# Three small edits in a four-layer graph kernel: buffer offsets, the place of a layer norm, and the number format of one matmul

## The reference

```python
x = layernorm(x + L0(x))   # two graph attention layers (4 heads of 256), then h @ Wfc + bfc
x = layernorm(x + L1(x))   # hp = h @ weight; msgs = hp[src] * edge_weight; relu(segment_sum(msgs, dst))
x = layernorm(x + L2(x))   # edge messages of 16 x 32 values, summed by src, then two small linear maps
x = layernorm(x + L3(x))   # relu([x[src], x[dst]] @ W.T + b), summed by src
```

## Time and profile before

| what | value |
|---|---|
| median of 3 runs | 2313.13 us (2309.23 to 2315.16) |
| the profiled execution | 2313.32 us, span 2311.3 us, mean granted clock 0.990 |
| PE, PEld busy | 2244.8 us (97%), 1913.1 us (83%) |
| DVE, ACT, POOL busy | 64%, 44%, 41% |

### The profile page before, as it was taken

The page is one execution under the profiler, slowest core; times in us unless marked ns, Lnnn a source line. Parts: engine busy times, 40 slices in busy tenths (PEclk is TensorE's granted clock), DMA queues, the critical chain, the costliest instruction groups (busy, mean ns, idle before and its releaser), DMA issues.

```text
span 2311.3 us, 36469 instructions
## 1 busy us (share of the span) xinstructions
PE 2244.8 (97%) x12307; PEld 1913.1 (83%) x12307; DVE 1490.6 (64%) x4613; ACT 1020.4 (44%) x2044; POOL 946.3 (41%) x931
## 2 busy tenths in 40 slices
PE   7999999979999999999999999999999999999996
PEld 5878788868899888888999999988887777778785
DVE  7777778744766856665345665267676666677675
ACT  3982112222456622222225665334334665666444
POOL 2017637654222234366632222023545554552542
PEclk9999999989999999999999999999999999999998
DMA  6334566442477657785226665456667777676531
GB/s 207 138 137 136 145 197 201 143 140 95 149 233 251 239 173 267 259 278 201 85 83 214 230 235 197 135 193 215 207 207 232 246 238 236 213 229 209 166 118 64
DMA packets 192415, 435.82 MB, mean 189 GB/s; under 512 B 45607, under 2 KB 74542, under 8 KB 191694
## 3 DMA queue, kind: packets, MB, share of 16 engines
q1 hardware_dynamic: 126954, 249.08, 31.4%
q0 software_dynamic: 65296, 184.67, 25.5%
HBM read 242.68 MB, written 190.96 MB: 188 GB/s over the span
## 4 chain that ended last, share of the span: by engine, by line
PE 71%; DVE 4%; ACT 2%; issue 1%; DMA 1%; POOL 0%; DVEq 0%; ACTq 0%; SPq 0%; POOLq 0%
PE g_h_ps L2563 6%; PE g_h_ps L2580 6%; PE g_h_ps L2565 6%; PE g_h_ps L2564 6%; PE g_h_ps L2581 6%; PE g_h_ps L2582 6%; PE g_h_ps L2605 5%; PE g_h_ps L2607 5%; PE g_h_ps L2606 5%; PE g_t_ps L2542 5%; PE g_h_ps L1744 2%; PE g_h_ps L1742 2%; PE g_h_ps L1743 1%; PE g_sum_ps L989 1%; PE g_sum_ps L990 1%
## 5 line engine op out<-in xcount | busy, mean ns | idle before, releaser
L2697 ACT ACTIVATE g_act_t<-g_t_ps,g_b_col 128x256 f32<-128x256 f32 (+1 forms) x488 | 202.2, 466 | 421.3 <-PE g_t_ps L2542 417.4
L2580 PE MATMUL g_h_ps<-g_x_hi,held_w_hi 128*128 128x256 f32 x1216 | 353.0, 290 | 0.0
L2582 PE MATMUL g_h_ps<-g_x_hi,held_w_lo 128*128 128x256 f32 x1216 | 343.9, 283 | 0.0
L2581 PE MATMUL g_h_ps<-g_x_lo,held_w_hi 128*128 128x256 f32 x1216 | 343.8, 283 | 0.0
L601 DVE CUSTOM_DVE_ANT_0 g_prod<-g_h_sb,g_a_rows 128x256 f32<-128x256 f32 x632 | 224.1, 418 | 80.8 <-ACT g_h_sb L492 73.2
L2605 PE MATMUL g_h_ps<-fc_w_hi,g_x_hi 128*128 128x512 f32 x632 | 272.3, 431 | 3.3 <-DVE fc_z L2982 2.5
L2563 PE MATMUL g_h_ps<-held_w_hi,g_x_hi 128*128 128x512 f32 x656 | 265.2, 404 | 0.0
L2565 PE MATMUL g_h_ps<-held_w_hi,g_x_lo 128*128 128x512 f32 x656 | 256.8, 392 | 0.0
L2564 PE MATMUL g_h_ps<-held_w_lo,g_x_hi 128*128 128x512 f32 x656 | 256.3, 391 | 0.0
L423 PE MATMUL g_h_ps<-g_w_hi,g_x_hi 128*128 128x512 f32 x616 | 243.3, 395 | 11.3 <-DVE g_x_lo L587 7.7
L2607 PE MATMUL g_h_ps<-fc_w_hi,g_x_lo 128*128 128x512 f32 x632 | 250.3, 396 | 0.0
(11 more groups left out here) (400 smaller groups left out, 4919.3 us busy)
## 6 DMA issues: line engine op xcount, KB each, us to landing
h<-g_h_sb SPq DMA_DIRECT2D x120, 512.0 KB, 4.3
g_x_in<-in_dram SPq DMA_DIRECT2D x40, 512.0 KB, 4.0
h<-g_rows_own SPq DMA_DIRECT2D x40, 512.0 KB, 4.9
h_cols<-g_h_sb SPq DMA_DIRECT2D x38, 512.0 KB, 5.8
xb_rows<-in_dram SPq DMA_DIRECT2D x19, 1024.0 KB
xb<-xb_rows SPq DMA_DIRECT2D x19, 1024.0 KB
g_x_in<-h_cols SPq DMA_DIRECT2D x38, 512.0 KB, 6.3
g_x_in<-h SPq DMA_DIRECT2D x21, 512.0 KB, 5.4
```

The lines of the kernel that those rows point to most:

```text
L2580: pe.matmul(out, wh, xh, start=(k == 0), stop=False)
L2581: pe.matmul(out, wh, xl, start=False, stop=False)
L2582: last = pe.matmul(out, wl, xh, start=False, stop=(k == KC - 1))
```

## The change

It makes three edits. A buffer of 256 bytes or more per partition now starts at a multiple of 64 bytes. In L1, `root`, `normalize` (ACT) and `shifts` (DVE) move from the slot with remainder 0 to the slot with remainder 3 of the same step. In L2, the sum over edges becomes two single-pass float32r matmuls, of `msg_hi` and `msg_lo`; ACT makes the upper part in part 0 (`round_messages`), DVE the rest at the head of part 1 (`rest_messages`).

```diff
@@ Space.__call__
-        self.end = -(-self.end // 32) * 32
+        unit = 64 if 4 * math.prod(shape[1:]) >= 256 else 32
+        self.end = -(-self.end // unit) * unit
@@ PainnEdges
-        self.carried = sem("painn_carried")
+        self.hi_steps = sem("painn_hi_steps")
@@ PainnEdges.gather
-                pool.wait_ge(self.msg_done, 3 * (t - 3))
+                pool.wait_ge(self.msg_done, 4 * (t - 3) - 1)
@@ PainnEdges.sum_edges
-        pe.wait_ge(self.msg_done, 3 * t + 3)
+        pe.wait_ge(self.msg_done, 4 * t + 4)
         if t:
-            pe.wait_ge(self.carried, t)
             pe.wait_ge(self.sums_out, t)
-        pe.matmul(h.psum_ps, h.mask[:, t * P:(t + 1) * P].bitcast(F32), h.pmsg[:, :], start=True, stop=True).then_inc(self.summed, 1)
+        mask = h.mask[:, t * P:(t + 1) * P]
+        pe.matmul(h.psum_ps, mask, h.msg_hi[:, :], start=True, stop=False)
+        pe.matmul(h.psum_ps, mask, h.msg_lo[:, :], start=False, stop=True).then_inc(self.summed, 1)
@@ PainnEdges.copy_features
-            act.wait_ge(self.msg_done, 3 * t)
+            act.wait_ge(self.msg_done, 4 * t - 1)
@@ PainnEdges.carry, round_messages
-        act.wait_ge(self.msg_done, 3 * t + 3)
-        act.activation(h.pmsg[0:1, :], h.psum_ps[0:1, :], ACT.Copy).then_inc(self.carried, 1)
+        act.wait_ge(self.msg_done, 4 * t + 3)
+        act.activation(h.pmsg[0:1, :], h.psum_ps[0:1, :], ACT.Copy).then_inc(self.hi_steps, 1)
+
+    def round_messages(self, act, t):
+        h = self.hold
+        act.wait_ge(self.msg_done, 4 * t + 3)
+        if t:
+            act.wait_ge(self.hi_steps, 2 * t)
+        act.activation(h.msg_hi[:, :], h.pmsg[:, :], ACT.Copy).then_inc(self.hi_steps, 1)
@@ PainnEdges.rest_messages
+    def rest_messages(self, dve, t):
+        h = self.hold
+        dve.wait_ge(self.hi_steps, 2 * t + 1)
+        dve.tensor_tensor(h.msg_lo[:, :], h.pmsg[:, :], h.msg_hi[:, :].bitcast(F32),
+                          ALU.subtract).then_inc(self.msg_done, 1)
@@ node_layers
+    def conv_late(g):
+        n, r = divmod(g - CONV, PACE)
+        return n - 2 if r == 3 and 0 <= n - 2 < ET else None
...
+        p.msg_hi, p.msg_lo = mid("msg_hi", [P, 10 * F], F32R), mid("msg_lo", [P, 10 * F], F32R)
@@ scalar, beside(g)
-                        if 0 <= n < ET:
-                            conv.root(act, n)
-                            conv.normalize(act, n)
+                    n = conv_late(g)
+                    if n is not None:
+                        conv.root(act, n)
+                        conv.normalize(act, n)
...
                             painn.carry(act, n + 1)
+                        if 0 <= n + 1 < ET:
+                            painn.round_messages(act, n + 1)
@@ vector, beside(g)
                             conv.factors(dve, n)
-                            conv.shifts(dve, n)
+                    n = conv_late(g)
+                    if n is not None:
+                        conv.shifts(dve, n)
...
                     if part == 1:
+                        if 0 <= n + 1 < ET:
+                            painn.rest_messages(dve, n + 1)
```

## The result

| what | before | after |
|---|---|---|
| median of 4 runs each | 2312.50 us (2309.23 to 2315.16) | 2329.39 us (2324.72 to 2330.77) |
| ratio, 95% interval | | 1.0070 (1.0057 to 1.0082) |
| the profiled execution, span | 2313.32, 2311.3 us | 2329.66, 2328.0 us |
| mean granted clock | 0.990 | 0.985 |

The changed kernel is slower, by 16.9 us between the medians and by 16.3 us between the two profiled executions. The forecast was 2309.4 us (2296 to 2321).

What follows compares the result with a forecast made beforehand. PE, busy 97% of the span, bounds the kernel. Edits of -7.0, -4.5 and +7.8 us sum to -3.7 us against 2313.3 us, 2309.6; the median lies 0.2 lower, so 2309.4 us, range 2296 to 2321.

Steps and rivals of the forecast that it cites:

- edit 1: FC and attention sums: operands at multiples of 64 bytes bring matmuls closer together, -7.0 us (bounds 0 and 15.2 us).
- edit 2: L1: later normalization lets ACT work in idle time; half of PE's 6.0 + 2.5 us waits goes, -4.5 us.
- shorter matmuls of the sum: L2's sum on PE: two single-pass matmuls save 0.22 us in each of 20 tiles, 4.4 us (3.6 to 5.2).
- wait on DVE's subtraction: L2: PE's sum waits for DVE's late subtraction, 2.0 us in each of 7 tiles, +14 us (8.4 to 20.3).
- `features`' wait given back: L2: in the late tiles ACT's copy no longer delays the next features; 1.8 of 2.0 us returns.
- clock at the new waits: PE's granted clock at L2's new waits: the prediction had no term for it.
- the price is 234.5 - 227.1 = 7.4 ns for a matmul: FC's step against the first attention product's: each misaligned matmul costs 7.4 ns, counted for 950 of FC's matmuls, 7.0 us.
- Rival C: FC's slow matmuls: the offset is not the cause, place in SBUF may be; edit 1 gives nothing, 2316.4 us; chance 0.14.
- half of 6.0 + 2.5: PE's waits on L1's rests (6.0 us) and on add_rows (2.5 us): half goes with edit 2, taken as -4.5 us.
- the wait on `add_rows`, of which half was to go: PE's single 2.5 us wait on DVE's add_rows beside L1 and L2, counted in edit 2's half.
- seven late tiles at 2.0 us: L2: DVE reaches part 1 late in 7 of 20 steps, at 2.0 us each, 14 us.
- the 1.03 us that the prediction needed: L2, part 1: DVE's idle time must cover 0.43 + 0.5 + 0.1 us of rounding and subtraction for edit 3 to be free.

Runs made afterwards that it cites:

- e1_offsets_only: Kernel before with edit 1 alone, large buffers at multiples of 64 bytes: 2312.95 us, ratio 1.0008.
- e2_late_only: Kernel before with edit 2 alone, L1's root, normalize and shifts three slots later: 2309.37 us, ratio 0.9993.
- e4_unit128: Kernel before with large buffers (512 bytes of a partition and more) at multiples of 128 bytes instead of 32: 2301.92 us, ratio 0.9963.
- e9_both_32: Kernel before with x's parts in the second product and FC moved to 32 past a multiple of 128, fc_w still 32 past one: 2308.52 us, ratio 0.9984.
- e6_rest_early: Changed kernel with DVE making the rest of the messages right behind the messages instead of three slots later: 2310.73 us, ratio 0.9980 to the kernel before.
- e5_shift64: Kernel before with every buffer moved up by 64 bytes: 2313.99 us, ratio 0.9996.
- e12_fc_up224: Kernel before with fc_w and the high buffers that follow it moved up by 224 bytes: 2310.53 us, ratio 0.9991.
- e10_best: Kernel before with large buffers at multiples of 128 bytes, edits 2 and 3, early rest, and sums copied ahead of softplus: 2301.32 us, ratio 0.9958.
- e3_sum_only: Kernel before with edit 3 alone, L2's sum as two single-pass matmuls of upper part and rest: 2327.50 us, ratio 1.0067.

## Why the prediction was wrong

| term | forecast, us | measured, us | read from |
|---|---|---|---|
| edit 1 | -7.0 | -0.2 | FC's first 960 matmuls; `e1_offsets_only` agrees |
| edit 2 | -4.5 | -2.3 | L1 in the trace; `e2_late_only`: -2.2 |
| shorter matmuls of the sum | -4.4 | -5.0 | 1.00 to 0.75 us in 20 tiles |
| wait on DVE's subtraction | +14.0 | +16.5 | PE's waits |
| `features`' wait given back | -1.8 | -1.3 | 2.0 to 0.7 |
| clock at the new waits | none | +7.9, an estimate | half of 17.1 - 1.4 us at half clock |

The measured terms make +15.6, against 16.3 between the executions. The terms of L2 make 18.1 of its 19.5 us; the 1.4 us between them, like the -1.2 and +1.0 us outside, are open.

**Edit 1 failed in the step "the price is 234.5 - 227.1 = 7.4 ns for a matmul".** The size was right: with the operands at a good distance FC's last tile steps 227.3 ns apart and FC's loop is 6.6 us shorter (`e4_unit128`). The condition was wrong. I compared the offset of the moving operand alone in two stages and took what differed there for the cause. In the fast stage weights and x also stand at the same offset modulo 256; in FC they are 160 apart, and edit 1 made that 192. Reading two offsets instead of one would have shown this second candidate ahead of any run. Rival C had the outcome, edit 1 worth nothing, but its cause, the place, fell with `e4_unit128` and `e9_both_32`. The Trainium skill's page "SBUF — State Buffer", section Specifications (TRN2), gives lines of 16 bytes. By them edit 1 was worth nothing, and `e1_offsets_only` (ratio 1.0008) agrees; but they don't explain what moving `fc_w` by 96 bytes in `e4_unit128` gave, so the measurement stands. Another page of the Trainium skill, "TensorE: Matmul & The Clock Gate", section "Step-by-step: what each phase is for", calls the two reads of the operands independent; the table above shows all the same that the distance between the two changes how fast matmuls follow each other.

**Edit 2** went as put, at half its size (and half of 6.0 + 2.5 is 4.25, not the 4.5 of the prediction): PE's waits on the rests fell from 6.0 to 3.3 us, ACT's wait of the root (now L1257) from 49.1 to 31.9 us, and the wait on `add_rows`, of which half was to go, only from 2.5 to 2.3.

**Edit 3's wait was right in kind and in size.** In tile 13 the forecast had 2.9 us and the trace shows 2.87; tile 11 has 1.17 against 1.2. I had counted seven late tiles at 2.0 us, there are eleven, of 1.5 us each; the two errors went opposite ways, so that 14.0 lies near 16.5 is in part luck. Six of the seven are among the eleven (tiles 3, 7, 10, 11, 13 and 19); the seventh late step comes behind the last sum. The average of 1.8 us in the earlier trace rows hides the shortest idles. In the kernel before, DVE's part 1 in the steps of tiles 5 and 17:

```profile
1996.78 0.29 DVE L1621 SCALAR_TENSOR_TENSOR painn_z<-g_h_ps,painn_z 128x128 f32<-128x128 f32 x1 [0.30 <-PE g_h_ps L1495]
...
2093.94 0.29 DVE L1621 SCALAR_TENSOR_TENSOR painn_z<-g_h_ps,painn_z 128x128 f32<-128x128 f32 x1 [0.29 <-PE g_h_ps L1495]
```

Both idles are below the 1.03 us that the prediction needed, and PE waits in both tiles. In the steps of tiles 0 and 1 there is no L1621 to read, and both wait (2.0 and 0.3 us). Why tile 15 waits 0.4 us, with 1.53 us of idle time before, is open.

**The term that was missing** is what the waits do to TensorE's clock. The prediction charged each wait its own length and gave no reason for leaving the clock out. Here two waits of 3.4 and 2.9 us came with 10.2 and 6.8 us at 1.2 GHz, and these 6.3 us of waiting cost some 7.9 us more. `e6_rest_early` takes the waits away and with them all but 3.4 us of the half clock.

With edit 1 at nothing and the clock in, the sum of the prediction would have been -3.7 + 7.0 + 7.9 = +11.2 us; the rest is mostly edit 2 and the longer wait. Neither alone would have led out of the range (2296 to 2321), both together did.

## What to carry to other kernels

Where a family of matmuls with 512 moving columns steps a few ns slower than another of the same shape, compare the offsets of both operands, modulo 256, not of one: one line in the allocator was worth 0.4% here, where the three edits together cost 0.7%. Where an instruction on a queue shared with other work becomes the last input of a matmul, put it right behind what makes its data; and price a wait of a busy TensorE of 3 us at more than its length, since the clock may fall behind it.

## What was not expected of the hardware

- **Two operands at a distance.** Far behind transposes (right behind them all step slower), single-pass matmuls with 512 moving columns step 226 to 227 ns apart where the moving and the stationary operand start at the same offset modulo 256, and 232 to 235 ns at distances of 128, 160, 192 and 224. Other distances and the reason were not tried.
- **With 256 columns it is the other way round.** In the second product's 256-column matmuls x is the moving operand. Twenty steps in the kernel before (alike) and in `e9_both_32` (32 apart):

```profile
702.13 0.28 PE L2580 MATMUL g_h_ps<-g_x_hi,held_w_hi 128*128 128x256 f32 x1
...
704.53 0.28 PE L2582 MATMUL g_h_ps<-g_x_hi,held_w_lo 128*128 128x256 f32 x1
```

```profile
699.96 0.28 PE L2581 MATMUL g_h_ps<-g_x_hi,held_w_hi 128*128 128x256 f32 x1
...
702.31 0.28 PE L2583 MATMUL g_h_ps<-g_x_hi,held_w_lo 128*128 128x256 f32 x1
```

  2.40 against 2.35 us, 120.0 and 117.5 ns: here the distance is the faster one, over 3,648 matmuls. Only this kernel shows it, and in these matmuls it doesn't tell the distance from the place of x. No kernel was built to use both.
- **The clock after short idles.** The granted clock fell to half at or just behind idles of PE of 3.4, 2.9 and, in `e6_rest_early`, 1.3 us, but not behind the 2.5 us of PE's wait on `add_rows` in the kernel before. Behind that same wait 3.4 us of half clock do follow in `e1_offsets_only`, `e5_shift64`, `e12_fc_up224` and `e10_best`; and tile 19's wait of 2.5 us in `e3_sum_only` is followed by it, that of 2.6 us in the changed kernel is not. A wait of such a length may or may not bring it.
